# One-tile loads, and scatters of GpSimd paced by landings, in the expert stage of an attention and routed feed-forward kernel

## What is computed

```python
x = x + attention(layernorm(x)) + ffn(layernorm(x))     # x: 16 batches x 512 tokens x 256
# ffn: 16 experts of 256 -> 128 -> 256, and a shared pair 256 -> 512 -> 256
scores = sigmoid(x @ gate.T)                      # 4 groups of 4 experts, the best 2 groups count
topk_idx = top_k(masked, 4)[1]                    # four experts for a token
topk_w = 2.5 * w / (w.sum(-1) + 1e-20)            # their weights
up = einsum('th,ehi->eti', x, expert_up)
down = einsum('eti,eih->eth', silu(up), expert_down)
moe_out = einsum('te,eth->th', combine, down)     # weighted sum over the four experts
```

## Time and profile before

| | |
|---|---|
| median of 3 runs | 972.61 us (971.91 to 973.69) |
| the profiled execution, its own time | 966.78 us |
| its span | 964.8 us |
| busy in the span: PE, DVE, ACT, POOL | 80%, 73%, 57%, 60% |
| mean granted TensorE clock | 0.929 |

### The profile page before, as it was taken

How to read it: one execution, slowest core, us unless ns; L and a number is a source line. 1 busy time by engine, 2 the same in 40 slices (tenths; PEclk the granted TensorE clock), 3 DMA queues, 4 the chain that set the end, 5 groups by cost and what they waited for, 6 DMA issues and landing times. The chain is left out here.

```text
span 964.8 us, 19765 instructions
## 1 busy us (share of the span) xinstructions
PE 768.8 (80%) x5264; PEld 704.2 (73%) x5264; DVE 700.7 (73%) x2390; ACT 553.1 (57%) x1142; POOL 581.4 (60%) x581
## 2 busy tenths in 40 slices
PE   4999999999999999997377767687676776776760
PEld 4899999999899988886266666676675775765750
DVE  5989898888888999999466555665556665656550
ACT  5677677676677766663155545554545544555440
POOL 1067766666777766666556565665555566656662
PEclk9999999999999999999599899998889888999795
DMA  5245554554445433332599888888887887888889
GB/s 156 71 171 193 186 176 179 194 187 175 149 159 188 146 129 129 114 116 112 177 288 284 239 266 266 252 261 268 245 252 250 270 267 247 265 264 261 249 277 304
DMA packets 142316, 202.15 MB, mean 210 GB/s; under 512 B 16176, under 2 KB 117184, under 8 KB 142208
## 3 DMA queue, kind: packets, MB, share of 16 engines
q1 hardware_dynamic: 114144, 116.47, 41.8%
q0 software_dynamic: 28064, 84.43, 22.8%
HBM read 104.19 MB, written 105.04 MB: 217 GB/s over the span
## 5 line engine op out<-in xcount | busy, mean ns | idle before, releaser
L574 POOL DMA_INDIRECT rows_by_expert<-xn,f_id x286 | 279.8, 978 | 194.4 <-issue 64.5
L490 POOL DMA_INDIRECT rows_by_expert<-xn,slots_now x192 | 196.9, 1026 | 122.8 <-PE bank_a L316 59.1
L1245 DVE TENSOR_TENSOR xt_l<-bank_a,xt_h 128x512 fp32r<-128x512 f32 x143 | 98.3, 687 | 97.1 <-ACT xt_h L698 67.4
L719 ACT ACTIVATE hid<-bank_x 128x256 f32<-128x256 f32 x143 | 55.3, 387 | 147.3 <-PE bank_x L316 71.5
L698 ACT CAST xt_h<-bank_a 128x512 fp32r<-128x512 f32 x143 | 83.8, 586 | 77.7 <-PE bank_a L1446 49.7
L316 PE MATMUL bank_y<-we,hs_h 128*128 x284 | 68.0, 333 | 68.4 <-DVE hs_l L1268 45.3
L316 PE MATMUL bank_a<-we,hs_h 128*128 x288 | 70.0, 337 | 61.9 <-DVE hs_l L1268 42.5
L316 PEld LDWEIGHTS bank_y<-we,hs_h 128*128 128x128 f32 x284 | 49.4, 210 | 82.3 <-issue 82.2
L316 PEld LDWEIGHTS bank_a<-we,hs_h 128*128 128x128 f32 x288 | 51.4, 216 | 75.0 <-issue 74.6
L316 PE MATMUL bank_y<-ws,hs_h 128*128 128x256 f32 x512 | 94.4, 282 | 1.4 <-DVE hs_l L997 1.4
L316 PE MATMUL bank_x<-xt_h,ws 128*128 128x512 f32 x256 | 92.1, 401 | 0.0
(11 more groups left out here) (289 smaller groups left out, 2427.7 us busy)
## 6 DMA issues: line engine op xcount, KB each, us to landing
xn<-rows_by_expert SPq DMA_DIRECT2D x215, 272.0 KB
x_in<-rows_by_expert SPq DMA_DIRECT2D x71, 272.0 KB
rows_by_expert<-spare SPq DMA_DIRECT2D x22, 544.0 KB
x_in<-in_L_attn_x_dram SPq DMA_DIRECT2D x16, 512.0 KB
out_dram<-rows_by_expert SPq DMA_DIRECT2D x8, 1024.0 KB
rows_by_expert<-xn,f_id POOLq DMA_INDIRECT x286
rows_by_expert<-xn,slots_now POOLq DMA_INDIRECT x256
w_raw<-in_L_ffn_expert_up_dram SPq DMA_DIRECT2D x32, 64.0 KB
```

Of the source, the lines that this page charges most:

```text
L490: G.indirect_dma_start(out=half_rows[:, :], in_=xn[:, c % NB, s, 0:RW], in_offset=None, out_offset=bass.IndirectOffsetOnAxis(ap=slots_now[ ...
L574: G.indirect_dma_start(out=half_rows[:, :], in_=f_y[u % YB][:, tile], in_offset=None, out_offset=bass.IndirectOffsetOnAxis(ap=f_id[:, u % ...
L719: S_.activation(f_hid[u % 2], X[u % 2][:, 0:UR], ACT.Silu).then_inc(fs_done, 1)
L1245: V.tensor_tensor(f_l[u % 4], A[u % 2][:, :].rearrange("p (c s t) -> p c s t", c=KD, s=2), f_h[u % 4].bitcast(F32), ALU.subtract).then_inc ...
```

## The change

Each load of the stage becomes two, of one tile each; both raise the same semaphore, and its readers wait for 32 in place of 16. The classes of units whose landings are counted fall from four to two, but each tile has a semaphore of its own, so SP still does four such waits a unit, with two values from the table in place of four. POOL's waits on `fd_done` and `fu_done` go; in their place a scatter waits for landings, so that no more than three are under way.

```diff
-    CLS = 4
+    CLS = 2
-        added = [sem(f"added{i}") for i in range(CLS)]
+        added = [[sem(f"added{k}_{tile}") for tile in range(2)] for k in range(CLS)]
-            return PRIMED + 32 * (u // CLS + 1)
+            return PRIMED + 16 * (u // CLS + 1)
-                    "(s p) r -> p s r", p=P)
+                    "(s p) r -> s p r", p=P)
-                sp.dma_start(f_rows[u % RB], unit_rows(row_of[u], 0)).then_inc(rows_loaded[u % RB], 16)
+                for tile in range(2):
+                    sp.dma_start(f_rows[u % RB][:, tile], unit_rows(row_of[u], 0)[tile]).then_inc(rows_loaded[u % RB], 16)
+
+            def landed(u):
+                for k in range(CLS):
+                    needed = four_from(mybir.EngineType.SP, 2 + k, u, PRIMED, PRIMED + 16 * UNITS)
+                    for tile in range(2):
+                        sp.wait_ge(added[k][tile], needed)
+                        sp.sem_inc(sums_free, 1)
...
                 if u >= YB:
-                    sp.wait_ge(added[(u - YB) % CLS], adds_until(u - YB))
-                for k in range(CLS):
-                    sp.wait_ge(added[k], four_from(mybir.EngineType.SP, 2 + k, u, PRIMED, PRIMED + 32 * UNITS))
-                    sp.sem_inc(sums_free, 1)
-                sp.dma_start(f_y[u % YB], unit_rows(row_of.pop(u), 1)).then_inc(acc_loaded[u % YB], 16)
+                    for tile in range(2):
+                        sp.wait_ge(added[(u - YB) % CLS][tile], adds_until(u - YB))
+                landed(u)
+                first_row = row_of.pop(u)
+                for tile in range(2):
+                    sp.dma_start(f_y[u % YB][:, tile], unit_rows(first_row, 1)[tile]).then_inc(acc_loaded[u % YB], 16)
...
-                pool.wait_ge(added[u % CLS], adds_until(u - CLS) if u >= CLS else PRIMED)
                 for tile in range(2):
+                    if u == 0:
+                        pool.wait_ge(added[0][tile], PRIMED)
+                        pool.wait_ge(added[1][tile], PRIMED)
                     if u >= 2:
-                        if tile == 0:
-                            pool.wait_ge(fd_done, min(u + 2, UNITS))
-                        else:
-                            pool.wait_ge(fu_done, min(u + 4, UNITS))
+                        pool.wait_ge(added[u % CLS][1], adds_until(u - 2))
+                    if u >= 1 and tile == 1:
+                        pool.wait_ge(added[(u - 1) % CLS][0], adds_until(u - 1))
...
-                    ).then_inc(added[u % CLS], 16)
+                    ).then_inc(added[u % CLS][tile], 16)
...
-                dve.wait_ge(rows_loaded[u % RB], 16 * (u // RB + 1))
+                dve.wait_ge(rows_loaded[u % RB], 32 * (u // RB + 1))
```

More of the change, by code:

```diff
@@ L410, in _ @@
             sp.wait_ge(scattered[(B - 3) % NB], scatters_until(B - 3))
-            sp.wait_ge(scattered[(B - 2) % NB], scatters_until(B - 2) - 16 * CLS)
+            sp.wait_ge(scattered[(B - 2) % NB], scatters_until(B - 2) - 16 * SUB)
             for k in range(CLS):
-                sp.wait_ge(added[k], PRIMED)
+                for tile in range(2):
+                    sp.wait_ge(added[k][tile], PRIMED)
             row_of = {}
@@ L442, in _ @@
                     load_sums(u - (ROWS_AHEAD - SUMS_AHEAD))
-            for k in range(CLS):
-                sp.wait_ge(added[k], four_from(mybir.EngineType.SP, 2 + k, UNITS, PRIMED, PRIMED + 32 * UNITS))
-                sp.sem_inc(sums_free, 1)
+            landed(UNITS)
             out_flat = out.rearrange("b s d -> (b s) d")
@@ L452, in _ @@
             for k in range(CLS):
-                sp.wait_ge(added[k], adds_until(UNITS - 1 - (UNITS - 1 - k) % CLS))
+                for tile in range(2):
+                    sp.wait_ge(added[k][tile], adds_until(UNITS - 1 - (UNITS - 1 - k) % CLS))
             sp.wait_ge(out_stored, 16 * PARTS)
@@ L498, in scatter_first @@
                     out_offset=bass.IndirectOffsetOnAxis(ap=slots_now[:, c % NB, s, 0:1], axis=0)
-                ).then_inc(added[s] if c == B - 2 else scattered[c % NB], 16)
+                ).then_inc(added[s // 2][s % 2] if c == B - 2 else scattered[c % NB], 16)
             pool.wait_ge(consts_made, CONSTS)
@@ L1132, in plan_rows @@
                 planned()
-                plan(V.tensor_scalar(u_class_n[:, :, :], u_class_i[:, :, :], 2, None, ALU.logical_shift_right))
+                plan(V.tensor_scalar(u_class_n[:, :, :], u_class_i[:, :, :], CLS.bit_length() - 1, None,
+                                     ALU.logical_shift_right))
                 planned()
-                V.tensor_scalar(u_tab[:, :, 2:2 + CLS].rearrange("p j k -> p k j"), u_class_n[:, :, :], 32.0, float(PRIMED), ALU.mult, ALU.add
+                V.tensor_scalar(u_tab[:, :, 2:2 + CLS].rearrange("p j k -> p k j"), u_class_n[:, :, :], 16.0, float(PRIMED), ALU.mult, ALU.add
                                 ).then_inc(plan_made, 1)
@@ L1249, in sum_up @@
                 expert = expert_from(experts, u)
-                dve.wait_ge(acc_loaded[u % YB], 16 * (u // YB + 1))
+                dve.wait_ge(acc_loaded[u % YB], 32 * (u // YB + 1))
                 V.tensor_tensor(f_id[:, u % YB, :], f_y[u % YB][:, :, bass.ds(expert + D, 1)].bitcast(U32)
@@ L1441, in turn_rows @@
             def turn_rows(u):
-                pe.wait_ge(rows_loaded[u % RB], 16 * (u // RB + 1))
+                pe.wait_ge(rows_loaded[u % RB], 32 * (u // RB + 1))
                 wait(pe, fx_lo, u - 1)
```

## The result

| | before | after |
|---|---|---|
| median, us | 973.15 (971.91 to 975.35, 4 runs) | 1039.82 (1033.78 to 1043.31, 4 runs) |
| ratio | | 1.0676, 95% interval 1.0622 to 1.073 |
| profiled execution, its span | 966.78, 964.8 | 1033.78, 1032.0 |

The account below looks back on a forecast made before the run. The prediction took the stage to be bound by engines waiting for one another, with scatter runs holding PE's signals. Stage 27.2, start +1.5 and end -2 gave +26.7 us, 999 on the median; range 942 to 1040.

Parts of the forecast that it names:

- 27.2 us: Expert stage: 143 units going from 3.23 to 3.42 us each add 27.2 us.
- +0.17 us a unit for the lost waits on PE: POOL's scatters in the stage: following their own sums, they make a unit 3.40 us, +0.17.
- SP as the bound: Rival, chance 0.18: four load DMAs and slow SP steps make units 3.5 to 3.8 us, total 1012 to 1054.
- the forecast's case: Stage with units 3.42 us apart and scatter runs of four; total 974.6 to 1012 us, chance 0.46.
- I take 0: One-tile loads on SP: 2.4 to 2.8 us a unit, under 3.42 and hidden by loads running ahead; cost 0.
- The cap seldom binds: POOL's cap of three: landings take 3.6 us, under the 3.80 of three scatters; 0.02 us a unit.
- The ends: Around the stage: first sums +1.5 us later from extra load issues; output copy starts earlier, -2 us.
- The weakest step: Stage: a run of POOL scatters holds PE's semaphores, delivered some 0.85 to 1.1 us after it stops.
- 6.47 us for two units: Kernel before, stage: 0.85 us restart, 4.77 of four scatters, 0.85 until held signals arrive; 3.23 a unit.
- the rhythm: Stage: PE's signals stick during POOL's run of four scatters and arrive 0.85 us after it ends.
- The faster rival: Stage: late landings break scatter runs and let PE's signals pass; units 2.8 to 3.1 us, 912 to 954, chance 0.29.

Follow-up runs that it names:

- e3: The kernel before without POOL's waits on PE (fd_done, fu_done) and without the cap; 855.84 us against 856.44 before, ratio 0.9989.
- e17: Repeat of e3, the kernel before without POOL's waits on PE; 855.60 us against 856.86 before, ratio 0.9973.
- e5_before_again: The kernel before, unchanged, run once more for a trace on a chip of the faster kind; 856.54 us.
- e11: The changed kernel with four scatters under way in place of three; 906.61 us against 856.63 before, ratio 1.0579.
- e2: The kernel before with one-tile loads alone; 926.87 us against 856.44 before, ratio 1.0823.
- e12: The changed kernel with the rows' loads whole again, the sums' loads of one tile; 987.58 us against 965.95 before, ratio 1.0226.
- e13: The changed kernel with the sums' loads whole again, the rows' loads of one tile; 988.41 us against 965.95 before, ratio 1.0222.
- e14: The changed kernel, unchanged, on the chip of e12 and e13; 1028.89 us against 965.95 before, ratio 1.0638.
- e8: The kernel before with 34 always satisfied waits a unit added on SP, loads whole; 929.95 us against 856.63 before, ratio 1.0858.
- e1: The changed kernel with all loads whole again, cap of three kept; 975.34 us against 856.44 before, ratio 1.1386.
- e7: The kernel before with 18 always satisfied waits a unit added on SP; 864.54 us against 855.40 before, ratio 1.0109.

## Why the prediction was right and wrong

- **Right by luck: that it gets slower.** Of the 27.2 us that the sum gives the stage 24 come from one term, +0.17 us a unit for the lost waits on PE, and the only kernels that lack these waits and nothing else aren't slower at all (e3 and e17, 0.9989 and 0.9973, on the first kind of chip; the other kind was not tried). The two terms that cost, the loads and the cap, stood in it at 0 and 0.02.
- **Right: how it would be seen.** POOL's scatters do start 1.1 to 1.2 us after their unit's sums (93 of 109 between 500 and 900 us), with waits put down to the sums. "Waits of PE or DVE on load DMAs, which there are none of now", and 3.5 to 3.8 us a unit, were the signs of SP as the bound: 164 us of such waits on PE, and 3.64. The rival with a chance of 0.18 is the one that fits the first pair; the forecast's case, 3.42 with runs of four scatters, did not come (87 of after's 100 runs are of one or two). (The waits alone prove little: in e5_before_again PE has 29.5 us of them in 280, while SP waits for 61.)
- **The step that failed: "I take 0" for the one-tile loads.** They were put at nothing because SP's time, 2.4 to 2.8 us a unit, was to hide under a unit of 3.42. The sum was near where nothing stumbles: 2.87 us in e11 ((873.9 - 466.2) / 142), the changed kernel's own loads with SP full, and 2.99 in e2 ((892.9 - 468.5) / 142), with its two table reads more. But there the rest of the stage needs 2.5 and not 3.42, so the loads cost 70 us. On the first pair's kind the sum itself is short: SP's slow steps, which rows 9 and 12 showed, had not been added. They are 0.35 us a unit at the least, and 0.35 + 0.41 = 0.76 if what the instructions that can wait lost (0.45, against 0.04 in e11) is not waiting either; then 2.87 + 0.76 = 3.63 is the measured unit of 3.64. One load less gives back 41 us (e12 and e13 against e14). The page "DMA: Bandwidth & Descriptors" of the Trainium skill, section "Rules for kernel authors", which asks to coalesce, points the right way: e2 agrees, 70 us, but through SP's issue time and not through the fixed cost of the transfers (e8). The section of the Trainium skill's page from which the prediction took 2.0 us is on DMAs issued by GpSimd, and these loads are SP's.
- **The cap, taken at 0.02 us a unit, was mis-sized.** "The cap seldom binds" set a landing after 3.6 us, with bounds of 2.79 and 4.4, against 3.80. The landing that is waited for takes 4.3 us under load, inside the bounds, but the 0.77 us from it to the next scatter was left out: 5.1 us against 3.8. Pacing alone is 119 / 143 = 0.83 us a unit on the first kind of chip. On the second, where unpaced scatters start 1.6 us apart, it wasn't tried by itself; together with a third load it makes 22 us. By the same page of the Trainium skill, section "Anatomy of one DMA — SWDGE (gpsimd) path", a scatter of 136 KB (139,264 bytes) would take about 2.0 + 0.3 = 2.3 us, an estimate; the quickest landings in e1, 2.4, agree, and the median of 4.0 does not, with DMA engines that are 0.79 busy.
- **The ends, taken at +1.5 - 2, were wrong in the second term.** The start is +1.6. At the end the copy does not start earlier against the last sums but 11.2 us later, since SP has no lead left, and 7.9 us are lost where 2 were to be won.
- **The weakest step, named as such, does not hold in general.** "PE's semaphores seem to be held while POOL scatters without a break": in e5_before_again POOL scatters almost without a break for the whole stage, and nothing is held. On the first pair's kind late signals do go with scatters, but not as the rhythm has it: of the 21 late casts 6 start in the midst of a scatter. So 6.47 us for two units was a rhythm that fitted the mean; that it is the cause isn't shown, and for the first kind it is refuted.
- **The faster rival fell with it**: landings break the runs in e1, and the unit goes from 2.51 to 3.30 us.
- **What stays open.** Why one kind of chip has SP moves of 0.7 us and late signals, with the same kernel; the runs only show it. And how the first pair's 66.7 us divide beyond the fourth load's 41: e1, e2 and e3 met no chip of that kind.

No version tried beats the kernel before by more than 0.3%.

## What to carry to other kernels

Before splitting transfers, add up the issuing queue's instructions for one step of the loop, slow ones with their share, and compare with the step; a queue that waits little is nearly full, and past that point each 0.1 us goes straight into the time. A queue that runs ahead also pays at the end of the stage: without its lead the last copy starts late. A cap on transfers under way costs nothing only while their number times the issue spacing is longer than a landing under load and the restart after it (here 4.3 + 0.8 us), both read under load. And when a wait on one engine follows work on another in a trace, look for the same pattern where that work is absent or denser, before a rhythm is built on it.

## What the runs showed of the hardware

- The same kernel takes 856 us on four chips and 966 to 973 on two occasions, on the latter with register moves of SP of up to 0.7 us (29 ns at the median) and starts of ACT up to 3.9 us behind finished work (21 of 102 over 1 us; 0 of 125 on the faster chips).
- An indirect scatter keeps POOL 0.96 us and the next starts after 0.30, with the DMA engines 0.85 busy (rows 2 and 5) and 0.99 busy at 330 GB/s alike.
- A scatter of 136 KB lands 2.4 us after its start at the least and 4.0 us at the median (e1); one that waited for it starts 0.77 us later.
- Satisfied waits on SP cost about 0.062 us for two: two on one instruction (e7, e8).
